# First expert FFN: computing all eight experts for every token, against sorting the tokens by chosen expert

## What is computed

```python
def _L0_ffn_ref(x, Wg, bg, W1, b1, W2, b2):       # D = 128, E = 8 experts; x is layer-normalised before
    logits = x_flat @ Wg + bg
    probs = jax.nn.softmax(logits, axis=-1)
    assignments = jnp.argmax(probs, axis=-1)
    h = jnp.einsum('nd,edh->neh', x_flat, W1) + b1[None]      # 128 x 128 per expert
    h = jax.nn.gelu(h, approximate=False)
    eo = jnp.einsum('neh,ehd->ned', h, W2) + b2[None]
    selected = jnp.take_along_axis(eo, assignments[:, None, None], axis=1)[:, 0, :]
    w = jnp.take_along_axis(probs, assignments[:, None], axis=1)
    return (w * selected).reshape(N, T, d)
```

## Time and profile before

| | us |
|---|---|
| median of 3 runs | 1609.48 (1606.61 to 1609.69) |
| the profiled execution's own time | 1610.01 |
| its span, first to last instruction | 1608.2 |
| attention of layer 0, one tile in the loop | 10.79 |
| last addition of attention to x, until layer 1's attention begins (372.46 to 527.93) | 155.5 |
| of it, one group of four tiles | 18.2 |

### The profile page before, as it was taken

The page is one execution under the profiler, slowest core; times in us unless marked ns, Lnnn a source line. Parts: engine busy times, 40 slices in busy tenths (PEclk is TensorE's granted clock), DMA queues, the critical chain, the costliest instruction groups (busy, mean ns, idle before and its releaser), DMA issues.

```text
span 1608.2 us, 51032 instructions
## 1 busy us (share of the span) xinstructions
PE 1458.7 (91%) x18049; PEld 1099.8 (68%) x18081; DVE 1174.6 (73%) x4888; ACT 915.9 (57%) x1793; POOL 610.6 (38%) x1180
## 2 busy tenths in 40 slices
PE   6999999997999588888788969998999999999998
PEld 5888888885666344555475636666777777788886
DVE  6777777875776699999946854443788998866664
ACT  5666665663555355555403335554578898865653
POOL 4555455541000466666306511111443434334331
PEclk9999999998999587878858979997999999999999
DMA  8000000004400000000002010000000000000000
GB/s 196 2 0 0 0 0 0 0 1 104 91 0 1 14 1 0 0 0 0 0 18 47 0 34 1 0 0 1 3 3 1 0 1 3 2 3 14 7 14 21
DMA packets 41756, 23.38 MB, mean 15 GB/s; under 512 B 23325, under 2 KB 39163, under 8 KB 41531
## 3 DMA queue, kind: packets, MB, share of 16 engines
q1 hardware_dynamic: 41658, 22.07, 6.0%
HBM read 17.87 MB, written 4.19 MB: 14 GB/s over the span
## 4 chain that ended last, share of the span: by engine, by line
PE 63%; DVE 20%; issue 8%; ACT 5%; POOL 3%; DVEq 1%; DMA 0%; SPq 0%; POOLq 0%; ACTq 0%
PE ps L681 8%; PE ps L690 7%; DVE arena L1354 5%; DVE arena L1348 4%; PE ps L310 3%; PE ps L352 3%; PE ps L2051 3%; PE ps L303 3%; PE ps L332 3%; PE ps L2058 3%; PE ps L2132 3%; PE ps L2045 2%; PE ps L343 2%; PE ps L323 2%; PE ps L1690 2%
## 5 line engine op out<-in xcount | busy, mean ns | idle before, releaser
L681 PE MATMUL ps<-xnT,arena 128*128 128x512 f32 x256 | 135.1, 620 | 0.0
L574 POOL TENSOR_TENSOR ln_veps<-ln_mv,eps 128x4 f32<-128x4 f32 x40 | 10.7, 269 | 269.2 <-DVE ln_mv L568 269.2
L2564 POOL TENSOR_TENSOR arena<-arena 128x512 f32<-128x512 f32 x64 | 67.8, 1060 | 111.1 <-DVE arena L2488 111.1
L1810 DVE TENSOR_SCALAR_CACHE_REDUCE thr_hits<-thr_abs,thr_candidate 128x512 bf16<-128x512 f32 (+1 forms) x248 | 101.8, 476 | 0.0
L1354 DVE MATCH_REPLACE8 arena<-arena 128x64 f32<-128x64 f32 x512 | 101.7, 208 | 0.1
L830 DVE SCALAR_TENSOR_TENSOR x_res<-ps,arena,x_res 128x128 f32 (+1 forms) x256 | 72.0, 344 | 31.1 <-PE ps L690 28.5
L530 POOL TENSOR_TENSOR arena<-arena 128x1024 f32<-128x1024 f32 x32 | 61.4, 1920 | 54.0 <-DVE arena L484 54.0
L469 DVE TENSOR_REDUCE arena<-ps 128x16 f32<-128x1024 f32 x32 | 39.2, 1224 | 57.7 <-PE ps L323 57.7
L690 PEld LDWEIGHTS ps<-arena 128*128 128x128 f32 x512 | 63.5, 191 | 25.5 <-issue 17.2
L1348 DVE MAX8 arena<-arena 128x8 f32<-128x64 f32 x512 | 76.1, 210 | 6.6 <-POOL arena L1235 5.4
L2051 PE MATMUL ps<-arena,toeplitz 96*128 96x128 f32 x512 | 71.6, 283 | 10.0 <-ACT arena L2283 4.8
(11 more groups left out here) (405 smaller groups left out, 4231.5 us busy)
## 6 DMA issues: line engine op xcount, KB each, us to landing
toeplitz<-ssm_toeplitz_scratch SPq DMA_DIRECT2D x2, 2048.0 KB, 17.9
ssm_toeplitz_scratch<-ssm_padded_kernel SPq DMA_DIRECT2D x1, 2048.0 KB, 11.3
out<-x_res SPq DMA_DIRECT2D x8, 256.0 KB, 2.3
arena<-ctx SPq DMA_DIRECT2D x2, 768.0 KB, 5.8
arena<-L_ffn_W SPq DMA_DIRECT2D x2, 512.0 KB
arena<-L_xattn_Wo SPq DMA_DIRECT2D x3, 256.0 KB, 8.8
arena<-L_xattn_Wq SPq DMA_DIRECT2D x1, 512.0 KB, 6.7
x_res<-x SPq DMA_DIRECT2D x1, 512.0 KB, 8.0
```

Source lines behind the costliest of these rows:

```text
L681: nc.tensor.matmul(ps[:, u % 3, :], w1[:, x, c * P:(c + 1) * P], xnT, start=True, stop=True).then_inc(h_full.sem, 1)
L1810: ins = V.tensor_scalar(self.hits[:, j, at:at + n], self.abs[:, at:at + n], self.cand[:, c:c + 1].bitcast(F32), 0.0, ALU.is_ge, ALU.add, a ...
L2564: G_.tensor_tensor(probs, probs, rc[:, s, :].unsqueeze(2).to_broadcast([P, heads, CTX]), ALU.mult).then_inc(s_prob.sem, 1)
```

## The change

`ffn0` is replaced by a class `RoutedExperts`. What it does:

- **During the attention loop**, two to four tiles behind it, every tile is normalised for the FFN (`dve_stats`, `dve_aggr`, `dve_apply`, `pool_rstd`), turned (`pe_turn`, `act_turn`), kept (`act_keep` into `xn_all`) and multiplied with the router (`pe_logits`, `act_logits`).
- **Per half** of 16 tiles: `dve_pick` finds the chosen expert as a one-hot; `pe_rank` counts with 17 matmuls how many tokens of the same expert come before each token; `dve_place` turns that into a row number in a buffer in HBM, where each expert's tokens fill whole blocks of 128 rows (24 blocks are enough for 16 tiles), and writes down which expert each block belongs to; `pool_scatter` writes the normalised rows there, one indirect DMA for each tile. For half 0 this happens in the loop (tiles 20 to 30), for half 1 behind it.
- **Behind the loop**, for each half, 6 chunks of 4 blocks: SP fetches 4 blocks (256 KB), PE turns them, multiplies with the block's own expert's W1, ACT does Gelu, PE multiplies with W2, DVE copies the result out of PSUM, SP stores it. `dve_experts` copies the weights of each block's expert into a two-slot buffer `wb`: it loads the expert's number from SBUF into a register and copies 128x257 values from an address that depends on it.
- **Last**, `pool_gather` fetches each token's row back with 16 indirect DMAs per half, and `dve_take` adds row times weight to x. The bias b2 stays as it was, group by group (`pe_bias`, `act_bias`, `dve_bias`).
- `dve_sum` now stands between the two halves in DVE's list, and the loads of layer 1's attention start as soon as the set-up is done. The attention loop has 4 tiles written out ahead of the loop and 12 behind it (2 and 2 before).

```diff
-def ffn0(k, io, freed):
-    return experts(k, io, "f0", True, 4, loads, freed, space, space, aside=k.ssm.dve_sum)
+class RoutedExperts:
...
@@ attention_heads, pe_step
             xn_turn(e, t + 1, o)
+            if past(t, 3):
+                route.pe_turn(e, t - 3, o, ps[:, 3, 256:384])
+            if past(t, 4):
+                route.pe_logits(e, t - 4, s, ps[:, 3, 384:384 + route.E])
             keys(e, t + 1, o)
             e.wait_ge(x_done.sem, x_done.at(t))
+            if is_at(t, RANK):
+                route.pe_rank(e, 0, ps[:, 2, 256:256 + route.E * (route.HALF + 1)])
...
@@ RoutedExperts
+    def pool_scatter(self, e, u):
+        p = u // self.HALF
...
+        e.indirect_dma_start(self.src[p][:, :], bass.IndirectOffsetOnAxis(self.pos[:, u:u + 1], 0), self.xn_all[:, u, :], None).then_inc(
+            self.scattered[p].sem, 16)
+    def pe_chunks(self, e, p):
...
+        turn(0)
+        for c in range(self.CHUNKS):
+            hidden(c)
+            if c + 1 < self.CHUNKS:
+                turn(c + 1)
+            if c:
+                outputs(c - 1)
+        outputs(self.CHUNKS - 1)
+    def dve_experts(self, e, p, c, ids):
+        V, n = self.k.nc.vector, p * self.CHUNKS + c
+        e.wait_ge(self.o_full.sem, max(n - 1, 0))
...
+        for j in range(GT):
+            x = e.value_load(self.expert[0:1, p, GT * c + j:GT * c + j + 1], min_val=0, max_val=self.E - 1)
+            last = V.tensor_copy(self.wb[:, GT * (n % 2) + j, :], self.w[:, bass.ds(x, 1), :].rearrange("p a n -> p (a n)"))
+        last.then_inc(self.w_laid.sem, 1)
+    def dve_chunk(self, e, p, c):
+        V, n = self.k.nc.vector, p * self.CHUNKS + c
+        e.wait_ge(self.o_full.sem, n + 1)
...
+        V.tensor_copy(self.out[:, c % 2, :, :].rearrange("p j d -> p (j d)"), self.k.ps[:, 4 + n % 2, :]).then_inc(self.o_laid.sem, 1)
+        if c + 2 < self.CHUNKS:
+            self.dve_experts(e, p, c + 2, None)
+    def dve(self, e):
...
+        self.dve_experts(e, 0, 0, None)
+        self.dve_experts(e, 0, 1, None)
+        self.dve_pick(e, 1)
+        self.dve_place(e, 1)
+        for c in range(self.CHUNKS):
+            self.dve_chunk(e, 0, c)
+        for g in range(GROUPS // 2):
+            self.dve_bias(e, g)
+        k.ssm.dve_sum(e)
+        self.dve_experts(e, 1, 0, None)
+        self.dve_experts(e, 1, 1, None)
+        for c in range(self.CHUNKS):
+            self.dve_chunk(e, 1, c)
+        self.dve_weigh(e, 1)
+        for u in range(self.HALF):
+            self.dve_take(e, u)
...
```

More of the change, by code:

```diff
@@ L70, in pipelined_tiles, with routed_tiles @@
     for t in range(TILES - tail, TILES):
+        step(t, t % 2)
+def routed_tiles(eng, step):
+    for t in range(4):
+        step(t, t % 2)
+    with eng.Fori(2, 10) as it:
+        step(2 * it, 0)
+        step(2 * it + 1, 1)
+    for t in range(20, TILES):
         step(t, t % 2)
@@ L235, in setup, with attention_heads @@
     return dict(pool=pool, pe=pe, act=act), (sp, sp_x, sp_rest), dict(pe=late_pe, act=late_act, dve=late_dve, pool=late_pool)
-def attention_heads(k, io, weights, gate, rounds, ssm, late):
+def attention_heads(k, io, weights, gate, rounds, ssm, late, route):
     nc = k.nc
@@ L289, in more, with past, is_at @@
         return not isinstance(t, int) or t + ahead < TILES
+    def past(t, lag):
+        return not isinstance(t, int) or t >= lag
     def is_first(t):
         return isinstance(t, int) and t == 0
+    PICK = route.HALF + 4
+    RANK, PLACE = PICK + 1, PICK + 2
+    def is_at(t, n):
+        return isinstance(t, int) and t == n
     def xn_turn(e, t, s):
@@ L428, in act_step @@
             gate_bias(e)
+        if past(t, 4):
+            e.wait_ge(route.l_full.sem, t - 3)
+        elif past(t, 3):
+            e.wait_ge(route.xt_full.sem, t - 2)
         if more(t, 1):
             xn_copy(e, t + 1, o)
+        if past(t, 3):
+            route.act_turn(e, t - 3, o, ps[:, 3, 256:384])
+        if past(t, 4):
+            route.act_logits(e, t - 4, ps[:, 3, 384:384 + route.E])
+        if is_at(t, RANK):
+            route.act_rank(e, 0, ps[:, 2, 256:256 + route.E * (route.HALF + 1)])
+        if past(t, 3):
+            route.act_keep(e, t - 3, o)
+        if is_at(t, RANK):
+            route.act_exp(e, 0)
+        if more(t, 1):
             keys_copy(e, t + 1)
@@ L474, in dve_step @@
             ln_aggr(e, t + 2, s)
+        if past(t, 2):
+            route.dve_aggr(e, t - 2, s)
         if is_first(t):
@@ L490, in dve_step @@
             rounds.dve_count(e, t)
+        if is_at(t, PICK):
+            route.dve_pick(e, 0)
+        if is_at(t, PLACE):
+            route.dve_place(e, 0)
+        if is_at(t, PLACE + 1):
+            route.dve_weigh(e, 0)
         if is_first(t):
@@ L525, in pool_step @@
             ln_pool(e, t + 2, s)
+        if past(t, 2):
+            route.pool_rstd(e, t - 2, s)
         if is_first(t):
@@ L534, in pool_step @@
         ssm.pool_pair(e, t)
+        if is_at(t, 1):
+            route.pool_constants(e)
+        if isinstance(t, int) and t > PLACE:
+            for u in range(2 * (t - PLACE - 1), min(2 * (t - PLACE), route.HALF)):
+                route.pool_scatter(e, u)
         if is_first(t):
```

404 lines of the change are left out of this document (384 added, 20 removed).

## The result

The changed kernel took 1673.48 us (median of 4, 1664.99 to 1676.65) against 1609.59 us for the kernel before beside it: a ratio of 1.039, 95% interval 1.034 to 1.044. The forecast was 1656 us, 46 us slower; it came out 64 us slower at the median, and 55 in the profiled execution (1664.99 us, span 1663.0), which is the fastest of the four and the one that can be followed.

A forecast was written before the change was run, and what follows sets the result against it. PE was taken to bound attention and the FFN. Attention grows 16.2 us and the serial chain behind it takes 185.5 us against 155.5, 30.0 more: together 46.2 on a median of 1609.5, so 1656 us, range 1616 to 1700.

The forecast's parts named there:

- the clock: Behind attention PE works in bursts at the 1.2 GHz level, granted clock 0.50, paying 1.9 times as much per record.
- the loop's tiles: Attention loop: PE's added transpose and router product cost 0.37 us in each of 29 tiles, 10.6 us.
- Attention: Attention gets 16.2 us longer: 10.6 for tiles, the rest for rank, ACT's copy behind it and the pick.
- Taken up by POOL: Attention: half 0's scatters, two per tile, are absorbed by POOL, busy 21 of 40 us.
- The price of a block: DVE's weight copies: register load, three register steps and unhidden copy take 1.2 us per block, 48 blocks on the path.
- The closed loop: Expert chunks: output copy, weight copies, hidden, turn and outputs run without overlap, 10.7 us per chunk, four times per half.
- The bias of half 0: Behind half 0's chunks: four groups at low clock, 3.6 us each, and the last addition 0.7, together 15.1 us.
- The last landing: End of the FFN: half 1's last gather lands 2.3 us after 16 gathers on POOL taking 19.2 us.
- Short loads, low clock: Rival, weight copies: 0.4 us per block with PE's clock still low, 1618 us; chance 0.06, shared with partial cases.
- POOL as the later engine: Rival, last gathers: an indirect DMA takes 2.4 us, +19.2, 1675 us; chance 0.24 shared among three rivals.
- long loads: Rival, weight copies: 2.0 us per block, 38 us more, 1694 us; chance 0.24 shared among three rivals.
- a failed cover in attention: Rival, attention: PE waits 1 us per tile for new ACT copies, +29, 1685 us; chance 0.24 shared among three.

The follow-up runs named there:

- second measurement: The changed kernel measured again without edit, against the kernel before, on a chip without unexplained engine stops: 1639.09 us, ratio 1.017.
- run 10: The changed kernel with the clearing of the HBM rows, and the loads behind it, moved into attention's loop: 1667.53 us, ratio 1.034.
- run 1: The kernel before with only attention's tile loop written out as in the changed kernel: 1613.50 us, ratio 1.002.
- first profile: Profile of the changed kernel's first result, its fastest execution of four: 1664.99 us, span 1663.0.
- runs 2 to 5: The changed kernel with half 0's scatters behind attention, 1652.74 us; without scatters, 1640.54; with Toeplitz transfers behind the gathers, 1630.50; unchanged, 1639.09.
- run 4: The changed kernel with SP's Toeplitz transfers (sp_matrices) held until half 1's last gather: 1630.50 us, ratio 1.013.
- Run 7: The changed kernel with Toeplitz transfers behind the gathers, plus a ring of three chunks of weights instead of two: 1614.58 us, ratio 1.002.
- runs 9 to 12: The changed kernel unchanged, 1673.16 us; with clearing moved into the loop, 1667.53; the reordered three-chunk kernel with rows fetched early, 1620.27; both edits, 1618.80.
- run 11: The reordered kernel with three chunks of weights, plus SP fetching rows early, ahead of the wait for outputs: 1620.27 us, ratio 1.003.
- run 8: The kernel with late Toeplitz transfers and three chunks of weights, plus serial pieces put beside other work: 1597.40 us, ratio 0.991.

## Why the prediction came out as it did

**What bounds the kernel, the clock, the loop's tiles: right.** A tile in the loop takes 11.12 us against 10.79, +0.33 (0.37 forecast), without gaps in PE; the rank tile 16.2, 5 us over the pace (5.6 with the pick), and the one behind it 13.1. In the second measurement most of those last 1.9 us are won back in the next two tiles (10.8 and 10.2). The granted clock fell to 0.5 to 0.65 behind attention.

**Attention, short by 6 to 9.5 us without stops, by 19.5 to 25 with them.** The step that failed is the sum itself: it counted instructions and never asked where the new code runs. In the second measurement the third addition comes at 67.83, against 59.02 before: 8.8 us late ahead of the loop. 2.0 of them are there at the first addition; the clearing and the loads behind it are up to 3.9 (run 10), the written-out shape as such 1.6 (run 1); the rest, 1.3 us, was not taken apart. From there to the last addition it is 16.9 us longer, and 16.2 had been forecast. In the first profile the start costs 5.6 us and the rest 30.1: the other 13 lie in the tiles with two scatters each. "Taken up by POOL" held on the chips without stops (runs 2 to 5: 329.8 to 330.4 us from the third addition to the last, with scatters and without) and not on the others, where PE pauses in the middle of a set. One tile of the first result, PE:

```profile
326.11 0.35 PE L363 MATMUL ps<-arena 64*64 64x64 f32 x5 [0.32 <-issue]
326.84 0.35 PE L363 MATMUL ps<-arena 64*64 64x64 f32 x6 [0.38 <-issue]
327.57 1.04 PE L363 MATMUL ps<-arena 64*64 64x64 f32 x51 [0.38 <-issue]
```

and the same set in run 4, scatters in place, chip without stops:

```profile
324.50 1.16 PE L363 MATMUL ps<-arena 64*64 64x64 f32 x64
```

**The price of a block (0.81 us for 1.2): the largest mis-sized term, 48 times 0.4, 19 us.** The prediction named it as the one to doubt, and said that below 0.8 it would be wrong in kind; at 0.81 it stayed slower. It shows in the 10.7 us from attention's end to the pick (13.5 forecast), in the chunk of 8.4 us, and ahead of half 1.

**The closed loop: right, and it is why the change loses.** Run 7 opened it, and a chunk fell from 8.4 us to between 7.1 and 7.6, where the rows hold it. The bias of half 0 was put too long (11 us for 15.1): it overlaps the last outputs.

**Indirect DMAs: right** in price (1.25 to 1.27 us apart, 1.2 forecast).

**The last landing: 13.7 us for 2.3.** The prediction saw `sp_matrices` beside the gathers and gave it "some us" that its sum leaves out. Run 4 priced it: 12.5 us.

**The rivals.** "Short loads, low clock" (1618, chance small) had the right pieces: its price of 0.4 us a block is too low; with the measured 0.81 the prediction's sum is 1637. That the second measurement, 1639, lies beside it is luck as well, since the landing and attention's start are still left out of it and other terms are too long. On POOL an indirect DMA kept 0.94 to 0.97 us beside DVE's weight copies. POOL as the later engine, long loads and a failed cover in attention did not happen. The mechanism that added most on two chips, the stops, was no rival at all. So 46.2 us came near to the first profile's 59.6 because errors of both signs met, which is luck: 31 us too many (19 for blocks, the rest, not measured one by one, in rank, bias and overlaps at each half's ends), against 11 us for the landing, 27 of stops (13 in attention, 14 behind it: 136.4 less 122.5) and 6 at the start that it didn't have.

**What stays open.** Why ACT and DVE stop, and PE pauses, beside POOL's indirect DMAs in some measurements. Shown: the stops occur on one chip out of three, and in the first result; there in every kernel (runs 9 to 12). ACT or DVE is idle for 5 to 18 us, mostly 8 to 14, beside or just behind a row of 16 indirect DMAs, also ones that gather and whose rows nobody waits for, and where I followed it, 3 to 12.5 us of that with all inputs there; PE's long waits behind attention are waits for what these two owe it. They strike code that runs once, but no indirect DMA lies beside a loop, so that this is needed is not shown. Argued only: that an engine's instructions arrive late because POOL's descriptors or rows are ahead of them. The instruction queues don't bear it out as they did for the third tile: in the first result a packet of 8 KB landed at 435.83, just ahead of ACT's stop from 435.86 on, and none followed before DVE ran again at 452.87. So the cause stays open. The kernels without scatters or with late ones ran on a chip without stops, so the indirect DMAs as the cause were not tried where it matters, nor was run 11 on a chip without stops. By run 8's ratio and its 26 us of waits for rows it should lie well below 0.991 there; that is an estimate.

## What to carry over

Ask of added work not only how long it takes but where its code runs: here straight-line code beside heavy transfers was 2.2 to 3.9 us slower and the loop beside the same transfers not at all. In a serial chain through four engines, find the one step that closes the loop; moving the Toeplitz transfers behind the gathers, giving the weights one more buffer and putting the serial pieces beside other engines' work turned 1.017 into 0.991 on one chip, while the same matmuls were computed. And before comparing a variant with a first result, run the first kernel again on the variant's chip: of the 43 us that run 4 seemed to gain, 34 were the chip or the hour.

## What was not expected of the hardware

- The kernel without indirect DMAs took 1609.6 to 1612.4 us on every chip; the one with them 1639 on one and 1673 on two occasions. The difference is in PE's pauses of 0.3 to 0.4 us and stops of ACT and DVE, mostly 8 to 14 us, with no releaser in the profile.
- 3 MB written at 249 GB/s, and the loads behind them, cost a loop nothing (11.12 us per tile) and code on its first pass 2.2 to 3.9 us. At one place of that code PE stood until 1.3 to 1.5 us after a 16 KB packet of an instruction queue had landed; it stood there for 1.3 to 1.5 us without the traffic and for 1.9 to 3.8 us beside it.
- A register load on DVE with its three register steps and a copy of 257 columns takes 0.76 us, of which the load 0.31.
- 16 gathers of 128 rows landed 1.6 us after POOL was done with the last of them with quiet queues, and 13.7 to 14.1 us after it beside 6 MB of other transfers.
